# RWKV mixing and a top-1 expert layer on one core: the output projection as rounded products, averages and shifts on ScalarE

## The reference

```python
# x: (4, 1024, 512); H = 512, 8 experts; all fp32
x_prev = shift(x, 1)                       # one step back in time, zero at the start
xk, xv, xr = (x_prev + (x - x_prev) * m for m in (tmk, tmv, tmr))
k, v, r = xk @ Wk.T + bk, xv @ Wv.T + bv, xr @ Wr.T + br
wkv = scan over time of (aa, bb, pp)       # weighted mean of v with weights exp(k), decaying
out = (sigmoid(r) * wkv) @ Wo.T + bo
x = layernorm(x + out)
logits = x @ wg;  e = argmax(logits);  gate = max(softmax(logits))
x = layernorm(x + gate * (x @ W[e].T + b[e]))
```

## Time and profile before

| what | value |
| --- | --- |
| median of 3 runs | 621.26 us (620.62 to 621.82) |
| the profiled execution | 622.48 us, its span 620.8 us |
| mean granted TensorE clock | 0.969 |
| busy share PE, PEld | 91%, 68% |
| busy share DVE, ACT, POOL | 87%, 69%, 44% |
| instructions | 9016 |

### The profile page before, as it was taken

The page is one execution under the profiler, slowest core; times in us unless marked ns, Lnnn a source line. Parts: engine busy times, 40 slices in busy tenths (PEclk is TensorE's granted clock), DMA queues, the critical chain, the costliest instruction groups (busy, mean ns, idle before and its releaser), DMA issues. The chain is left out here.

```text
span 620.8 us, 9016 instructions
## 1 busy us (share of the span) xinstructions
PE 566.4 (91%) x2452; PEld 421.6 (68%) x2453; DVE 542.3 (87%) x862; ACT 428.8 (69%) x806; POOL 271.6 (44%) x217
## 2 busy tenths in 40 slices
PE   0786788999999999999999999999998999999991
PEld 0565565667668767776866876786466878788880
DVE  6978898999999899899999989899999699777770
ACT  4636475577767759767766865966886777788872
POOL 2165454461454445355245454512032364756631
PEclk9888889999999999999999999999996999999996
DMA  8273063028108404701910840477654576877740
GB/s 299 111 184 86 1 167 37 1 83 216 42 1 231 110 0 175 146 18 40 246 51 0 226 112 2 149 188 273 180 190 151 174 235 210 260 229 226 233 157 0
DMA packets 40980, 84.41 MB, mean 136 GB/s; under 512 B 8751, under 2 KB 8751, under 8 KB 40818
## 3 DMA queue, kind: packets, MB, share of 16 engines
q1 hardware_dynamic: 30482, 56.67, 27.4%
q0 software_dynamic: 10464, 27.33, 19.7%
HBM read 66.95 MB, written 35.65 MB: 165 GB/s over the span
## 5 line engine op out<-in xcount | busy, mean ns | idle before, releaser
L1110 POOL TENSOR_TENSOR mixed<-unsplit,mixed 128x1024 fp32r<-128x1024 f32 x44 | 106.4, 2439 | 149.4 <-ACT mixed L762 149.4
L516 PE MATMUL kb<-mixed,w_kvr 128*128 128x512 f32 x384 | 98.4, 407 | 20.7 <-DVE w_kvr L1450 14.1
L516 PE MATMUL vb<-mixed,w_kvr 128*128 128x512 f32 x384 | 101.6, 415 | 10.9 <-DVE evn L1292 10.8
L692 PE MATMUL y_ps<-w_e_hi,xgT 128*128 x312 | 109.0, 411 | 0.1
L516 PE MATMUL rb<-mixed,w_kvr 128*128 128x512 f32 x384 | 100.3, 411 | 4.7 <-DVE ee L1306 4.7
L529 PE MATMUL y_ps<-w_o,rw 128*128 128x512 f32 x224 | 100.8, 594 | 0.0
L516 PEld LDWEIGHTS kb<-mixed,w_kvr 128*128 128x128 f32 x384 | 73.7, 195 | 39.5 <-issue 13.8
L516 PEld LDWEIGHTS vb<-mixed,w_kvr 128*128 128x128 f32 x384 | 73.4, 196 | 32.3 <-DVE evn L1292 14.3
L516 PEld LDWEIGHTS rb<-mixed,w_kvr 128*128 128x128 f32 x384 | 73.0, 192 | 26.2 <-DVE ee L1306 5.9
L1126 POOL TENSOR_TENSOR ee<-ee,state 128x512 f32<-128x512 f32 x32 | 34.9, 1091 | 91.7 <-DVE state L1276 90.9
L1243 DVE SCALAR_TENSOR_TENSOR unsplit<-diff,vec,xb 128x512 f32<-128x512 f32 x96 | 65.8, 747 | 6.4 <-PE kb L516 6.1
(11 more groups left out here) (230 smaller groups left out, 1020.2 us busy)
## 6 DMA issues: line engine op xcount, KB each, us to landing
bias<-b_experts SPq DMA_DIRECT2D x39, 256.0 KB, 4.5
x_biased<-bo POOLq DMA_DIRECT2D x8, 1024.0 KB, 17.3
w_e_raw<-w_experts SPq DMA_DIRECT2D x8, 1024.0 KB, 7.9
rows<-x_biased SPq DMA_DIRECT2D x28, 256.0 KB, 3.6
x_rows<-rows SPq DMA_DIRECT2D x28, 256.0 KB, 6.6
xb<-xT SPq DMA_DIRECT2D x4, 1026.0 KB, 5.3
xb<-xT SPq DMA_DIRECT2D x3, 1024.0 KB, 5.2
w_raw<-w_square SPq DMA_DIRECT2D x2, 1024.0 KB, 10.8
```

Of the source, the lines that this page charges most:

```text
L516: mm = pe.matmul(bank, w_kvr[m][:, a, h, o:o + P], mixed[m][:, bb, h, :], start=(k == 0), stop=(k == 3 * CH - 1))
L692: mm = pe.matmul(y_ps[:, n % 2, :], xgT[n % 3][:, a, c, :], w[:, bass.ds(p, 1), c, :].rearrange("p u o -> p (u o)"), start=(c == 0 and (a, ...
L1110: pool.tensor_tensor(mixed[m][:, LO, 2 * hp:2 * hp + 2, :], unsplit[m][:, LO, 2 * hp:2 * hp + 2, :], mixed[m][:, HI, 2 * hp:2 * hp + 2, :] ...
```

## The change

- The output weight and the result are each split into a high and a low part; an output tile is twelve products of F32R operands in place of four of fp32. ScalarE rounds (`result_hi`, and the weight once), VectorE subtracts (`result_lo`, `out_weight_lo`). The reciprocal and the result are made in the place of the low part; pair 0 has two buffers in turn, pair 1 has one, and the last pair of block 7 has its own, where `xb` was. So `reciprocal_guess` now waits for output tiles, and `result` no longer does.
- In the blocks `average` and `shift` leave VectorE. ScalarE does them in `deviation` (a copy with a scale), and likewise the shift in `norm2`.
- Block 7 starts two output tiles with their first half (`out_first`) before the second pair is ready.
- Expert e is in place e. Experts are loaded and rounded in another order, 6 and 7 after the last output tile; the second table of `tile_experts` and its register loads go.

```diff
+            def out_pair(bank, half, p, j):
+                for c in range(2 * p, 2 * p + 2):
+                    hi, lo = (part[half, p][:, c % 2, j * P:(j + 1) * P] for part in (rw_hi, rw_lo))
+                    w_lo_c = w_o_lo[c // 3][:, c % 3, :]
+                    pe.matmul(bank, hi, w_o[:, c, :], start=(c == 0), stop=False)
+                    pe.matmul(bank, hi, w_lo_c, start=False, stop=False)
+                    mm = pe.matmul(bank, lo, w_o[:, c, :], start=False, stop=(c == CH - 1))
+                return mm
...
-                for c in range(CH):
-                    mm = pe.matmul(y_ps[:, j % 2, :], rw[:, half, c, j * P:(j + 1) * P], w_o[:, c, :],
-                                   start=(c == 0), stop=(c == CH - 1))
+                for p in range(PAIRS):
+                    mm = out_pair(y_ps[:, j % 2, :], half, p, j)
...
-            out_last(0)
+            out_first(0)
+            out_first(1)
+            out_second(0)
             turn_rows(before, 0)
-            out_last(1)
+            out_second(1)
...
+            def result_hi(i, half, p):
+                act.wait_ge(rw_raw, i * 2 + (p + 1))
+                act.activation(rw_hi[half, p][:], er[half, p][:], ACT.Copy).then_inc(rw_rounded, 1)
...
             def deviation(n, h):
                 two = slice(2 * h, 2 * h + 2)
+                act.wait_ge(y_taken, n * TPB + (2 * h + 4))
+                act.activation(mean[:, two], row_sum[:, two], ACT.Copy, scale=-1.0 / H).then_inc(stats_done, 2)
...
                 act.activation(rstd[:, two], rstd[:, two], ACT.Exp, scale=-0.5).then_inc(rstd_ready, 1)
+                act.wait_ge(rstd_ready, n * 2 + (h + 1))
+                act.activation(nmr[:, 2 * h:2 * h + 1], mean[:, 2 * h:2 * h + 1], ACT.Copy, scale=rstd[:, 2 * h:2 * h + 1])
+                act.activation(nmr[:, 2 * h + 1:2 * h + 2], mean[:, 2 * h + 1:2 * h + 2], ACT.Copy,
+                               scale=rstd[:, 2 * h + 1:2 * h + 2]).then_inc(nmr_ready, 1)
...
                 enter_ab(i, 1, *here)
+                if s.prev:
+                    result_hi(m, 1 - s.half, 1)
                 if s.prev2:
                     move_turned(m2, 1)
...
                 enter_ab(i, 3, *here)
+                result_hi(i, s.half, 0)
                 mix_hi(i + 1, V, 0)
...
             deviation_before(0)
+            result_hi(last, END, 1)
             norm(before, 0)
             act.wait_ge(r_filled, CHUNKS)
+            expert_hi(1)
             expert_hi(2)
-            expert_hi(3)
...
             move_turned(before, 3)
+            expert_hi(5)
...
             move_gathered(1, 1)
-            act.wait_ge(y_filled, TILES)
+            expert_hi(6)
             expert_hi(7)
...
+            def result_lo(i, half, p):
+                dve.wait_ge(rw_rounded, i * 2 + (p + 1))
+                dve.tensor_tensor(rw_lo[half, p][:], er[half, p][:], rw_hi[half, p][:].bitcast(F32), ALU.subtract).then_inc(wkv_done, 1)
...
                 distance(i, 1)
-                if s.prev2:
-                    shift(m2, 1)
                 if s.prev:
...
                     result(m, 1 - s.half, 1)
+                else:
+                    out_weight_lo()
...
                 distance(i, 2)
+                if s.prev:
+                    result_lo(m, 1 - s.half, 1)
                 difference(i + 1, s.batch + 1 if s.half == 1 else None)
...
                 distance(i + 1, 0)
+                result_lo(i, s.half, 0)
                 if s.prev:
-                    shift(m, 0)
                     add_rows(m, 2)
...
                 denominator(i, 3)
-                if s.prev:
-                    average(m, 1)
...
             recurrence(last, 3)
+            result_lo(last, END, 0)
             add_rows(before, 0)
...
             add_rows(before, 2)
+            result_lo(last, END, 1)
             early_columns()
...
-            load_experts((6, 7))
             store_rows(last - 1, range(TPB))
+            sp.wait_ge(y_filled, TILES)
+            load_experts((6, 7))
```

More of the change, by code:

```diff
@@ L72 @@
 HI, LO = range(2)
+END = HALVES
 SQ, SA, SB = range(3)
@@ L147, in build @@
         evn = place("evn", [P, 2, 2, TB], F32)
-        er = place("er", [P, 2, 2, TB], F32)
+        pair = 4 * 2 * TB
+        first_at = cursor[0]
+        cursor[0] += 2 * pair
+        rw_hi_at = {(0, 0): first_at, (0, 1): rw_at, (1, 0): rw_at + 2 * pair, (END, 1): xb_at}
+        rw_hi = {hp: place(f"rw_hi{hp[0]}{hp[1]}", [P, 2, TB], F32R, at=at) for hp, at in rw_hi_at.items()}
+        rw_lo = {hp: place(f"rw_lo{hp[0]}{hp[1]}", [P, 2, TB], F32R, at=at + pair) for hp, at in rw_hi_at.items()}
+        er = {hp: place(f"er{hp[0]}{hp[1]}", [P, 2, TB], F32, at=at + pair) for hp, at in rw_hi_at.items()}
+        for parts in (rw_hi, rw_lo, er):
+            parts[1, 1] = parts[0, 1]
+            parts[END, 0] = parts[1, 0]
         e2 = place("e2", [P, 2, TB], F32)
@@ L753, in _ @@
                     turn(k + 2, (k + 2) // RING, (k + 2) % RING)
[L754 removed]
+                ahead = expert(k, k % RING, ahead[0], ((expert_mixed, m + 1),) if m + 1 < MIXED else ())
         @block.scalar
@@ L1014, in _ @@
             enter_ab(last, 1, *here)
+            result_hi(before, 0, 1)
             move_turned(earlier, 2)
@@ L1046, in _ @@
             norm(before, 1)
+            expert_hi(3)
+            move_turned(before, 1)
             expert_hi(4)
-            move_turned(before, 1)
-            expert_hi(5)
-            act.wait_ge(y_filled, last * TPB)
-            expert_hi(6)
             deviation_last(0)
@@ L1590, in _ @@
             recurrence(last, 0)
-            shift(earlier, 1)
             running_max(last, 1)
             distance(last, 1)
-            try_guess(before, 1)
-            refine(before, 1)
+            try_guess(before, 0, 1)
+            refine(before, 0, 1)
             result(before, 0, 1)
@@ L1602, in _ @@
             distance(last, 2)
+            result_lo(before, 0, 1)
             dve.wait_ge(mixed_f32, BLOCKS * 6)
@@ L1613, in _ @@
             early_ranks()
-            try_guess(last, 0)
-            refine(last, 0)
-            result(last, 1, 0)
+            try_guess(last, END, 0)
+            refine(last, END, 0)
+            result(last, END, 0)
             cap_gate(last, 2)
@@ L1628, in _ @@
             gates(0, EARLY, gate_e, 1)
-            try_guess(last, 1)
-            refine(last, 1)
-            result(last, 1, 1)
+            try_guess(last, END, 1)
+            refine(last, END, 1)
+            result(last, END, 1)
             add_rows(before, 2)
+            result_lo(last, END, 1)
             early_columns()
```

157 lines of the change are left out of this document (78 added, 79 removed).

## The result

The changed kernel takes 631.82 us in the median of 4 runs (630.73 to 634.29), the kernel before 621.54 beside it: a ratio of 1.0174 [1.0157, 1.0190], 10.3 us slower. The forecast was 627.4 us, slower; the time lies inside its range of 616 to 634, 4.4 us above the forecast. The profiled execution after took 631.99 us (span 630.3), 9.5 more than the one before, so the two traces can be set against each other stage by stage.

The account below looks back on a forecast made before the run. It took TensorE (52.4 us a block) and VectorE (50.5 without waits) as near the bound in blocks, TensorE alone in tiles. -2, +4.2 and +3.9 made +6.1 on 622.5, so 628.6, or 627.4 as median; range 616 to 634.

Parts of the forecast that it names:

- the blocks: All blocks together, without clock falls: -2 us, with -0.3 in each of five blocks and -0.8 in block 1.
- the clock: TensorE's clock falls behind the new gap at the logits, in three of five blocks at 1.4 us: +4.2 us.
- the passage: From the last block to the first expert product, where work added on VectorE goes straight to the end: +3.9 us.
- Output projection and floor: Output tiles go from 3.43 to 2.73 us on TensorE, but VectorE's own work holds a block at 50.7 us.
- fourth rival: The change gives TensorE's full 2.8 us a block, 605.6 us in all; excluded by VectorE's rows, no chance of its own.
- Waits in the block: In blocks, the turned-row copy queues behind the rounding: TensorE idles about 1.7 us, gate of chunk 1 comes 0.5 later.
- Rival 1: No clock falls in the blocks, since the gap is shorter or logits count: 623.2 us, chance 0.22.
- The head of block 7: Gate of chunk 0 in the last block comes later through ScalarE's longer queue: net +1.1 us.
- The way to the first product: Passage after the gate: subtractions +2.4, last result's rounding +0.5, expert 5's rounding +0.5, fewer small instructions -0.6 us.
- Experts 6 and 7: Loaded after the last output tile (about 464), rounded by 476: costs nothing, or 2 to 3 us if loads are slow.
- Rival 3: The new subtractions on VectorE wait for GpSimd, about 1 us in each of five blocks: 632 us, chance 0.05.
- Rival 2: ScalarE's copy of turned rows is in time, VectorE's floor is reached, blocks take 50.8 us: 616.7 us, chance 0.23.

Follow-up runs that it names:

- e5: Changed kernel with averages and shifts given back to VectorE in the blocks and ahead of the last block: 633.88 us, ratio 1.0209.
- e3: Changed kernel with TensorE's product of the gate's chunk 0 in block 7 ahead of the logits: 634.79 us, ratio 1.0150.
- g1: Changed kernel with the moves of e2 and e3, out_last(2) ahead of the list's products, expert 5's rounding ahead of deviation_last(0): 620.11 us, ratio 0.9984.
- h1: g1 without the move of e3, so TensorE's order at the head of the last block is the changed kernel's: 622.10 us, ratio 1.0010.
- f1: Kernel before with only the late loads of experts 6 and 7 and expert 6's rounding behind the second gathered tile: 626.41 us, ratio 1.0051.
- e2: Changed kernel with ScalarE's copy of turned tile 1 ahead of the rounding of the second pair, in the loop's blocks: 626.09 us, ratio 1.0089.
- f4: Kernel before with only the averages and shifts of the blocks and the shifts of the tiles moved to ScalarE: 620.16 us, ratio 0.9979.
- f3: e2 without the lower part of the results: no result_lo, eight products a tile for twelve: 623.22 us, ratio 1.0020.
- g3: f3 with averages and shifts back on VectorE in the blocks: 626.88 us, ratio 1.0092.

## Why the prediction was right in its sign and 4.4 us short

**Luck in the total.** The sum was -2 for the blocks, +4.2 for the clock and +3.9 for the passage. The runs show -3.65, +1.4 and +11.8 (3.26, 3.77 and 4.77). The passage cost three times its term; the time still lies in the range because the blocks and the clock were 4.45 us too dear and took back over half of that error of 7.9. So the profiled execution shows +9.5 where +6.1 was forecast, 3.4 us; the other 1.0 of the 4.4 is that the forecast took off 1.2 us from execution to median, where the changed kernel's two differ by 0.2.

**Output projection and floor: right.** The twelve products of a tile start 0.23 us apart (eleven of them from 439.77 to 442.09), 2.8 for the tile where 2.73 was forecast. VectorE's floor was put at 50.7 us a block, from the earlier trace rows; it is 50.2. TensorE was to be busy some 47 of 50 us; it is busy for 50.0 of a block's 51.98, which is 48.1 of 50. It does not give its 22 us, as the forecast said and its fourth rival did not.

**Waits in the block: right.** "TensorE, free at 250.1, idles about 1.7 us": the logits waited 1.47. The gate of chunk 1 still waits 0.67, that of chunk 2 waits 0.46 (forecast: half of 0.97 gained). A block of 52.1 was forecast, 51.98 came. Block 1 was forecast 0.8 shorter and came 1.1 shorter (51.09 for 52.17).

**The clock: the mechanism was right, the count was not.** The step was "a fall in three of five blocks at 1.4 us, +4.2". The profiled execution shows one in the five blocks, at 302.63 us, behind the same gap as its four neighbours (V took 4.58 us), and the blocks ended 2.25 us early instead of 2.2 late: of the 4.45 between, 2.8 are the count (one fall for three at 1.4), and 1.65 are blocks that win more than the -2 of the forecast: the fall at 82.78 of the kernel before didn't come here, and without the fall the later blocks win 0.5 each where 0.3 was forecast. The size of a fall held there (a block of 53.40 against 52.0). Rival 1 (no fall, 623.2) was nearer in the blocks and still lost, since the passage was not 3.9.

**The head of block 7: mis-sized.** "Net +1.1" for the gate of chunk 0; it was 3.26. The sum had ScalarE's longer queue in it, and short: the gate's product starts 8.19 us after the start of the block where it started 6.49 after, +1.7 for the +1.1. It did not have what TensorE does in the wait: it stands at the logits (of an earlier block's rows) for 2.90 us with the gate's product behind them, and then makes that product at half clock (4.58 for 3.0, +1.6). Each of two edits takes much of it away: with averages and shifts back on VectorE the cap comes 2.84 us earlier (e5), with the gate's product first 1.88 (e3), and this second one is worth 1.6 to 2.0 us of time (g1 against h1).

**The way to the first product: short by 1.** Forecast +2.8 after the gate (2.4 + 0.5 + 0.5 - 0.6), measured +3.77, of which 0.02 up to chunk 3. Two subtractions at 1.22 and a wait of 0.52 for the last rounding are as forecast. Expert 5's rounding was put at 0.5: VectorE waits 1.46 for it, because ahead of it ScalarE's copy of the last turned tile waits for TensorE, which had waited 1.70 for the list's operands and was then at half clock. Here the forecast looked at the instruction and not at what stands in front of it.

**Experts 6 and 7: the step that failed.** "TensorE needs the third tile's split only at about 487: nothing, and 2 or 3 us if the loads are slow." It was +4.77. The split of the third tile was indeed not what waited. ScalarE was: two roundings of 1.9 us and 3.87 us of waits stand ahead of the rows of the last block, whose logits stand in TensorE's order ahead of tile 2. Only VectorE's queue had been looked at. The loads were also later than the forecast had them: out at 468.88 for "about 464", both matrices rounded at 481.2 for "by 476". Before, the rounding of expert 6 stood where ScalarE still had 2.58 us to wait for the last block's rows. f1 shows some 3 us for this part alone in the kernel before; when the last output tile ends earlier, 2.9 of the 4.77 go in the profile of g1 and all of it in that of h1.

**Rivals.** Rival 3 (subtractions blocked by GpSimd, 632) gives the measured time, but not by its mechanism: 16 subtractions at 1218 ns. Rival 2 needed the copy to land before 250.9 and it decided indeed: with the copy first (e2) the block is 51.34 and 5.7 us are won, though not the 50.8 that the rival gave.

**Averages and shifts on ScalarE**, which the forecast had inside the same sum, are a small gain in the kernel before: 1.3 us (f4). In the changed kernel a gain is not shown (e5): what they give in the blocks they take at the head of block 7.

**What stays open.** The parts measured alone in the kernel before, +3.2 for the loads and -1.3 for the averages, leave 8.4 of 10.3 us for the projection in rounded parts and its order, if the parts add up, which was not shown. The moves of e2, h1 and g1 take away 11.7, so the cost is mostly one of order. But g1, with all of them, stands where f4 stands without any rounded projection (620.11 and 620.16 us; ratios 0.9984 and 0.9979): even in the better order no run shows that the rounded projection gains anything. Why f3's block stays at 50.9 us with no engine full was not settled: theory C expected 49, and theory D (ScalarE's queue), as it was put, was refuted by g3. The falls of the clock (6 in f3, none in e2) are at most a part of it: a block of f3 without a fall still took 50.9 to 51.0, and three with one at most 0.8 more. What the half clock in the passage costs by itself was not tried.

## What to carry to other kernels

When a change makes the engine at the bound faster, list for every wait that it newly meets what is queued behind the waiting instruction, on every engine, and who needs it: here three places of that kind (a rounding ahead of a copy, logits ahead of a gate, the list's products ahead of the output tile that the expert loads wait for) were the most of it: four moved calls took 11.7 us off. A buffer that is shared with something released later turns an early load into a late one; look for what the load's consumers are queued in front of, not only for who reads it. And test parts by themselves in the old kernel: the small one (averages on ScalarE) paid 1.3 us there, as much as the whole change in the best order that was tried.

## What the runs showed of the hardware that was not expected

The granted clock fell behind waits of TensorE of only 1.2 to 1.5 us (1.17 and 1.31 at the logits of f3 ahead of its products at 193.30 and 245.19, which took 4.58 and 4.43 us; 1.46 in the changed kernel ahead of 302.63), and the same wait in four neighbouring blocks of the changed kernel left it alone. At the head of block 7 TensorE waited 2.90 us in the changed kernel, 2.91 in e2 and 2.91 in h1; the product behind it took 4.58, 2.99 and 4.58 us. TensorE of e2 there:

```profile
396.44 1.06 PE L564 MATMUL lists_ps<-wgs,x1T 128*128 128x8 f32 x8 [2.91 <-ACT x1T L899]
...
397.74 2.99 PE L525 MATMUL rb<-mixed,w_kvr 128*128 128x512 f32 x12
```

So the length of a wait alone does not tell whether it costs the clock; a count of such waits gives a chance. Executions of one kernel may well differ by it (623.6 to 628.0 us in e2, 618.2 to 623.9 in g1, with mean clocks of 0.955 to 0.966, the fastest ones at the upper end), though only one execution of each was profiled. The two kernels with eight products a tile, f3 and g3, show 6 slow groups each between block 1 and the head of block 7, and mean clocks of 0.941 and 0.943 in their profiled executions; the other twelve have none to four and 0.951 to 0.971. So part of what a less busy TensorE could win there may be paid back in clock.
